# A grouped expert matmul: the first expert's loads in four buffers and on two queues, LoRA factors first, base loads later

## The reference, cut to what matters

```
w = weight[adapter_ids]
c = einsum('bsi,boi->bso', x, w)
h = einsum('bsd,nrd->nbsr', c, lora_A)
lora_out = einsum('nbsr,nor->bso', h, lora_B * (2 * lora_weights)[:, None, None])
return x + einsum('bsd,od->bso', c, W) + bias + lora_out
```

## Time and profile before

| | before |
|---|---|
| median of 3 runs | 1561.61 us (1561.08 to 1564.95) |
| profiled execution, its time | 1557.48 us |
| its span | 1555.8 us |
| TensorE busy (matmuls) | 1500.1 us, 96% |
| VectorE busy | 782.0 us, 50% |
| ScalarE busy | 386.7 us, 25% |
| POOL busy | 484.3 us, 31% |
| mean granted clock | 0.987 of full |

### The profile page before, as it was taken

How to read it: one execution, slowest core, us unless ns; L and a number is a source line. 1 busy time by engine, 2 the same in 40 slices (tenths; PEclk the granted TensorE clock), 3 DMA queues, 4 the chain that set the end, 5 groups by cost and what they waited for, 6 DMA issues and landing times.

```text
span 1555.8 us, 27863 instructions
## 1 busy us (share of the span) xinstructions
PE 1500.1 (96%) x6352; PEld 1197.8 (77%) x6353; DVE 782.0 (50%) x1183; ACT 386.7 (25%) x493; POOL 484.3 (31%) x656
## 2 busy tenths in 40 slices
PE   6779999999999999999699999999999999999998
PEld 3568788888887788887588888888888888888886
DVE  5477565675677575567773333333333333333330
ACT  3233343333334333333442101010010101010100
POOL 2743543335433334433321212121212121212221
PEclk9889999999999999999899999999999999999999
DMA  8887878778799877688866555555555555555553
GB/s 195 267 207 171 199 185 191 181 166 203 176 201 197 194 158 191 181 195 185 193 157 180 138 137 145 139 141 140 140 142 139 141 139 138 145 135 148 135 135 81
DMA packets 175346, 257.86 MB, mean 166 GB/s; under 512 B 22616, under 2 KB 131288, under 8 KB 175320
## 3 DMA queue, kind: packets, MB, share of 16 engines
q1 hardware_dynamic: 104368, 140.09, 39.2%
q10 hardware_dynamic: 50728, 72.37, 18.9%
q0 software_dynamic: 20224, 45.13, 9.9%
HBM read 181.99 MB, written 75.50 MB: 166 GB/s over the span
## 4 chain that ended last, share of the span: by engine, by line
PE 59%; issue 12%; DMA 10%; DVE 9%; ACT 3%; POOL 2%; SPq 2%; DVEq 2%; POOLq 1%; ACTq 1%
PE ps L668 20%; PE ps L670 19%; PE ps L669 19%; DMA w_raw<-in_L_cond_weight_dram 7%; DVE w_turn L487 3%; DVE w_lo L541 3%; DMA x_raw<-in_x_dram 2%; DVE x_turn L561 2%; ACT w_hi L370 1%; SPq L206 1%; POOL x_raw L193 1%; DVEq L182 1%; POOLq L182 1%; POOL fold_sb L322 1%; ACT x_hi L378 1%
## 5 line engine op out<-in xcount | busy, mean ns | idle before, releaser
L668 PE MATMUL ps<-w_hi,x_hi 128*128 (+1 forms) x2096 | 832.6, 397 | 30.8 <-ACT stage L396 13.1
L669 PE MATMUL ps<-w_lo,x_hi 128*128 (+1 forms) x2096 | 831.2, 397 | 0.0
L670 PE MATMUL ps<-w_hi,x_lo 128*128 (+1 forms) x2096 | 831.1, 397 | 0.0
L668 PEld LDWEIGHTS ps<-w_hi,x_hi 128*128 128x128 f32 x2096 | 395.4, 189 | 130.4 <-issue 23.9
L670 PEld LDWEIGHTS ps<-w_hi,x_lo 128*128 128x128 f32 x2096 | 395.1, 189 | 96.0
L669 PEld LDWEIGHTS ps<-w_lo,x_hi 128*128 128x128 f32 x2096 | 395.5, 189 | 95.5
L193 POOL DMA_DIRECT2D x_raw<-in_x_dram x560 | 300.3, 536 | 430.2 <-DVE x_turn L561 269.6
L378 ACT ACTIVATE x_hi<-x_turn 128x512 fp32r<-128x512 f32 x272 | 160.5, 626 | 798.1 <-DVE x_turn L561 475.0
L351 POOL TENSOR_TENSOR stage<-stage,w_raw 128x1024 f32<-128x1024 f32 x64 | 154.1, 2408 | 595.2 <-DMA stage<-in_x_dram 595.2
L561 DVE STREAM_TRANSPOSE x_turn<-x_raw 128x256 f32<-128x256 f32 x544 | 193.8, 414 | 177.9 <-DMA x_raw<-in_x_dram 141.5
L613 DVE TENSOR_TENSOR stage<-ps,stage 128x1024 f32<-128x1024 f32 x64 | 78.3, 1224 | 349.4 <-PE ps L670 349.4
(11 more groups left out here) (63 smaller groups left out, 27.0 us busy)
## 6 DMA issues: line engine op xcount, KB each, us to landing
w_raw<-in_L_cond_weight_dram SPq DMA_DIRECT2D x256, 256.0 KB, 5.8
y_scr<-stage ACTq DMA_DIRECT2D x144, 256.0 KB, 4.2
x_raw<-in_x_dram POOLq DMA_DIRECT2D x560, 64.0 KB, 3.2
x_raw<-y_scr SPq DMA_DIRECT2D x128, 256.0 KB, 2.7
stage<-in_x_dram SPq DMA_DIRECT2D x128, 256.0 KB, 3.7
out_dram<-stage ACTq DMA_DIRECT2D x128, 256.0 KB, 2.9
base_sb<-in_L_ffn_W_dram POOLq DMA_DIRECT2D x8, 512.0 KB, 8.9
weff<-fold_sb POOLq DMA_DIRECT2D x8, 512.0 KB, 5.4
```

The costliest lines, as they stand in the source:

```text
L668: mm(ps[b][:, cols], x_hi[b][:, t, :], hi, start=t == 0, stop=False)
L669: mm(ps[b][:, cols], x_hi[b][:, t, :], lo, start=False, stop=False)
L670: last = mm(ps[b][:, cols], x_lo[b][:, t, :], hi, start=False, stop=t == KT - 1)
```

## The change

Rank 0 gets four load buffers in place of two: the two `w_raw` and two more, `w0_raw`, which lie in memory that is used later (by `base_sb` 2 and 3, and by the last quarter of rank 1's `w_hi`, where folds 6 and 7 are put). Rank 0's loads, and the x of slots 0 and 1, are issued in two parts: partitions 0 to 63 (q = 0, 1) on SP's queue, and partitions 64 to 127 (q = 2, 3) on ScalarE's queue (loads 0 and 1) or POOL's (loads 2 and 3, and x). The row of ids moves from SP to ScalarE and the LoRA weights' coefficients from ScalarE to SP; B and A stand ahead of ScalarE's share of the loads. SP now also loads the x of slots 2, 3 and 4, ahead of rank 1's loads. POOL loads W (`load_base`) after x of slot 1, the third and fourth once six chunks are turned, and makes its eight additions without x loads between. ScalarE rounds no chunk ahead of the LoRA factor `bt_sb`, and alternates chunks and folds in another order. All experts' loads are issued in the order q = 0, 2, 1, 3.

```diff
-                   for i, at in enumerate((16, 20, 8, 12))]
+                   for i, at in enumerate((8, 12, 16, 20))]
+        w0_raw = [nc.alloc_sbuf_tensor_at(f"w0_raw{i}", [P, 2 * P // BLK, SEG], f32, offset=at)
+                  for i, at in enumerate((spare + 16 * D, base + EXPERT_BYTES + (FOLDS - 2) * 4 * D))]
...
+        first_raw = w_raw + w0_raw
...
+        def load_first(eng, c, quads, loaded):
+
+            rows = w[0][2 * c * P:2 * (c + 1) * P, :].rearrange("(m j) n -> j m n", j=BLK)
+            for q in quads:
+                eng.dma_start(first_raw[c][BLK * q:BLK * (q + 1), :, :],
+                              rows[:, :, q * SEG:(q + 1) * SEG]).then_inc(loaded[c], 16)
...
-                    if not (isinstance(k, int) and k == 0 and c < 2):
-
+                    if isinstance(k, int) and k == 1 and c < 2:
+
+                        sp.wait_ge(w_turned, 2 * (c + 1))
+                    else:
                         sp.wait_ge(w_turned, k * CHUNKS + 2 * (c - 1))
...
-                    for q in range(QUADS):
+                    for q in (0, 2, 1, 3):
...
-            sp.dma_start(row_i[:, :], ids.rearrange("(a s) -> a s", a=1).to_broadcast([P, SAMPLES])).then_inc(ids_loaded, 16)
-            load_expert(0, w[0], range(0, LOADS // 2))
+            sp.dma_start(coef[:, :],
+                         lora_weights.rearrange("(n a b) -> n a b", a=1, b=1).to_broadcast([NLORA, RANK, 1])
+                         ).then_inc(coef_loaded, 16)
+            for c in range(2):
+                load_first(sp, c, (0, 1), w0_loaded)
             sp.wait_ge(tables, 1)
             for h in range(2):
-                load_sample(sp, 0, 0, h, first_loaded[0])
-            load_expert(0, w[0], range(LOADS // 2, LOADS - 1))
+                load_sample(sp, 0, 0, h, first_loaded[0], (0, 1))
+            for c in range(2, LOADS):
+                load_first(sp, c, (0, 1), w0_loaded)
             for h in range(2):
-                load_sample(sp, 1, 1, h, first_loaded[1])
-            load_expert(0, w[0], range(LOADS - 1, LOADS))
+                load_sample(sp, 1, 1, h, first_loaded[1], (0, 1))
+            for n in range(2, RING + 1):
+                for h in range(2):
+                    load_sample(sp, n, n % 2, h, first_loaded[n % 2])
             sp.wait_ge(tables, 2)
             load_rank(1)
...
+            pool.wait_ge(tables, 1)
+            for h in range(2):
+                load_sample(pool, 0, 0, h, first_rest[0], (2, 3))
+            for c in range(2, LOADS):
+                load_first(pool, c, (2, 3), w0_rest)
+            for h in range(2):
+                load_sample(pool, 1, 1, h, first_rest[1], (2, 3))
             pool.wait_ge(b_turned, 1)
-            pool.wait_ge(x_turned, 2)
             for f in range(BASES):
+                if f == 2:
+                    pool.wait_ge(w_turned, 6)
                 load_base(f)
-            load_x(2, 0)
-            for f in range(0, 3):
-                add_base(f)
-            load_x(3, 1)
-            for f in range(3, 6):
+            for f in range(FOLDS):
                 add_base(f)
-            load_x(4, 0)
-            for f in range(6, FOLDS):
-                add_base(f)
-            load_x(5, 1)
+            load_x(RING + 1, 1)
...
-            act.dma_start(coef[:, :],
-                          lora_weights.rearrange("(n a b) -> n a b", a=1, b=1).to_broadcast([NLORA, RANK, 1])
-                          ).then_inc(coef_loaded, 16)
+            act.dma_start(row_i[:, :], ids.rearrange("(a s) -> a s", a=1).to_broadcast([P, SAMPLES])).then_inc(ids_loaded, 16)
...
+            for c in range(2):
+                load_first(act, c, (2, 3), w0_loaded)
...
-            round_w(0, 0, [0])
             act.wait_ge(b_turned, 1)
...
-            round_w(0, 0, [1])
-            move_fold(0)
-            round_w(0, 0, [2])
-            move_fold(1)
-            round_w(0, 0, [3])
+            for c in range(4):
+                round_w(0, 0, [c])
+                move_fold(c)
             round_x(0, 0)
-            move_fold(2)
-            move_fold(3)
-            round_w(0, 0, [4])
             move_fold(4)
-            round_w(0, 0, [5])
+            round_w(0, 0, [4, 5])
             move_fold(5)
-            round_w(0, 0, [6])
+            round_w(0, 0, [6, 7])
             move_fold(6)
-            round_w(0, 0, [7])
             move_fold(7)
...
             prepare_w(0, 0, range(0, CHUNKS // 2))
-            prepare_x(0, 0, 0, 0, [first_loaded], 2 * QUADS)
+            prepare_first(0)
             prepare_w(0, 0, range(CHUNKS // 2, CHUNKS))
-            prepare_x(1, 1, 1, 0, [first_loaded], 2 * QUADS)
-            for n in range(2, RING + 1):
-                prepare_x(n, n % RING, n % 2, n // 2 - 1)
+            for n in range(1, RING + 1):
+                prepare_first(n)
             prepare_w(1, 1)
```

More of the change, by code:

```diff
@@ L151, in grouped_adaln_ffn_kernel @@
         weff_ready = sem("weff_ready")
+        w0_loaded = [sem(f"w0_loaded{c}") for c in range(LOADS)]
+        w0_rest = [sem(f"w0_rest{c}") for c in range(LOADS)]
         w_loaded = [sem(f"w_loaded{b}") for b in range(2)]
@@ L157, in grouped_adaln_ffn_kernel @@
         first_loaded = [sem(f"first{b}_loaded") for b in range(2)]
+        first_rest = [sem(f"first{b}_rest") for b in range(2)]
         y_loaded = [sem(f"y_loaded{b}") for b in range(2)]
@@ L182, in entry, with load_sample @@
             return eng.value_load(table[:, bass.ds(i, 1)], min_val=0, max_val=top)
-        def load_sample(eng, n, b, h, loaded):
+        def load_sample(eng, n, b, h, loaded, quads=range(QUADS)):
             sample = entry(eng, slot_sample, 2 * n + h, SAMPLES - 1)
@@ L480, in turn_w @@
                 load, part = c // 2, c % 2
-                if part == 0:
-                    dve.wait_ge(w_loaded[load % 2], 16 * QUADS * (load // 2 + 1) + k * (16 * QUADS * LOADS // 2))
+                raw = w_raw[load % 2]
+                if isinstance(k, int) and k == 0:
+                    raw = first_raw[load]
+                    if part == 0 and load < 2:
+                        dve.wait_ge(w0_loaded[load], 16 * QUADS)
+                    elif part == 0:
+                        dve.wait_ge(w0_loaded[load], 16 * 2)
+                        dve.wait_ge(w0_rest[load], 16 * 2)
+                elif part == 0:
+                    dve.wait_ge(w_loaded[load % 2], 16 * QUADS * (load // 2 + 1) + (k - 1) * (16 * QUADS * LOADS // 2))
                 if not (isinstance(k, int) and k == 0 and c < TURN):
@@ L487, in turn_w @@
                 nc.vector.transpose(w_turn[c % TURN][:, :, :].rearrange("p t (m j) -> p m t j", j=BLK),
-                                    w_raw[load % 2][:, part * P // BLK:(part + 1) * P // BLK, :].rearrange("p m (t i) -> p m t i", i=BLK)
+                                    raw[:, part * P // BLK:(part + 1) * P // BLK, :].rearrange("p m (t i) -> p m t i", i=BLK)
                                     ).then_inc(w_turned, 1)
@@ L554, in prepare_x, with prepare_first, turn_x @@
                     dve.wait_ge(sems[raw], load * (16 * loads) + 16 * loads)
+                turn_x(n, b, raw)
+            def prepare_first(n):
+                dve.wait_ge(first_loaded[n % 2], (2 + 4 * (n // 2)) * 2 * 16)
+                if n < 2:
+                    dve.wait_ge(first_rest[n], 2 * 2 * 16)
+                turn_x(n, n % RING, n % 2)
+            def turn_x(n, b, raw):
                 for h in range(2):
@@ L576, in prepare_next_expert, with x_index @@
                     dve.nop()
+            def x_index(n):
+                return n // 2 - (2 if n % 2 else 3)
             prepare_w(0, 0, range(0, CHUNKS // 2))
[L579 removed]
+            prepare_first(0)
             prepare_w(0, 0, range(CHUNKS // 2, CHUNKS))
[L581 to L583 removed]
+            for n in range(1, RING + 1):
+                prepare_first(n)
             prepare_w(1, 1)
@@ L587, in _ @@
                 if slot > 1:
-                    prepare_x(n, n % RING, n % 2, n // 2 - 1)
+                    prepare_x(n, n % RING, n % 2, x_index(n))
                 prepare_next_expert(slot)
@@ L593, in _ @@
                     v = u + AHEAD
-                    prepare_x(slot + AHEAD, v % RING, v % 2, g * (RING // 2) + (v // 2 - 1))
+                    prepare_x(slot + AHEAD, v % RING, v % 2, g * (RING // 2) + x_index(v))
                     prepare_next_expert(slot)
```

## The result

The changed kernel took 1546.05 us (median of 4 runs, 1544.98 to 1547.09), the kernel before 1563.12 us beside it (4 runs, 1561.08 to 1564.95): ratio 0.9896, 95% interval 0.9882 to 0.991. The profiled executions stand closer together, 1557.48 and 1546.04 us (spans 1555.8 and 1543.9): before's was 5.6 us under its median, after's is on it. So 11.9 us can be followed in the traces.

What follows compares the result with a forecast made beforehand. TensorE bounds the kernel, so only its 55.7 us of standing still can be won. 21.7 us up to slot 55 (the preparation's 22.4 is larger) plus 2 before slot 67 make 23.7: 1561.6 - 23.7 = 1537.9 us, range 1529 to 1547.

Steps and rivals of the forecast that it cites:

- the later of two shifts: Whole run: TensorE and the preparation must both move early; the end shifts only by the later one's shift.
- the start up to half 0, and POOL: Slot 0 and Weff: half 0 starts at 30.2 instead of 30.52; POOL's additions end at 61.0 instead of 80.47.
- the order's size: Expert loads in order 0, 2, 1, 3: each W phase gets 0.65 us shorter.
- rival 1: Expert loads: the order gives nothing, leaving a gain of 17.2 us, 1544.4; chance 0.17.
- Rival 2: W phases: both load waits vanish, 3.5 us in each late phase; 32.2 us gained, 1529.4; chance 0.13.
- chunks 6 and 7 rounded at 39.8 and 40.9, the last `w_lo` at 42.2: Slot 0, rank 0's last chunks: ready for half 1 to start at 42.3, 8.0 us early.
- just in time: Rank 1's loads on SP: issued from 57.2 behind three x loads, landed at 66, with Weff ready at 66.5.
- my 87.2: End of rank 1's W phase: 20.7 us after Weff is ready at 66.5, shifting the preparation by 17.2 us.
- rival 3: Rank 1's loads become the wait: first lands 8 us late, phase ends at 95.2; 16.4 us gained, 1545.2; chance 0.13.
- the head: Stretch up to the end of rank 1's W phase: the preparation gets 17.2 us early there.
- fewer bytes are in flight: Argument against rank 1's loads becoming the wait: less traffic than at 50 to 58 us, when 386 GB/s moved.
- The offset: Whole run: the median of the runs is 4.1 us above the profiled execution, giving 1537.9 from 1533.8.

Runs made afterwards that it cites:

- f: Changed kernel with the eight additions done on VectorE, two behind each x of slots 1 to 4, not on POOL: 1545.07 us.
- k: Kernel before with only each expert load's order changed to 0, 3, 1, 2, which changes partition half each time: 1554.10 us.
- a: Kernel before with only each expert load's order changed to 0, 2, 1, 3: 1552.18 us.
- l: Kernel before with only each expert load's order changed to 1, 0, 3, 2, which keeps neighbours of one partition half: 1561.66 us.
- b: Changed kernel with the old order 0, 1, 2, 3 of each expert load, all else kept: 1554.47 us.
- e: Changed kernel with POOL's eight additions replaced by fills with zero, which write and don't read: 1542.02 us (1 run).
- c: Changed kernel with rank 1's first two loads issued on SP ahead of x of slots 3 and 4: 1538.62 us.
- d: Changed kernel with x of slots 3 and 4 issued on ScalarE's queue, behind the roundings of x 1 and 2: 1539.14 us.
- i: Changed kernel with rank 1's first two loads on SP right behind x of slot 1, ahead of x of slots 2 to 4: 1538.28 us.

## Why the prediction was right or wrong

**Right: that only idle time could move, and that the later of two shifts counts.** "The shift is that of the later one": half 1 moved by 2.5 us in after, 6.6 in f beyond that, and the run followed rank 1 instead. In all 14 kernels slot 6 starts 7.9 to 9.3 us after rank 1's phase ends.

**Right: the start up to half 0, and POOL.** `bt_sb` ran at 14.95 (predicted 14.4), folds from 16.12 (15.6), half 0 at 29.30 (30.2). The last addition ended at 60.41 (61.0), and Weff was no longer waited for.

**Right: the order's size.** Predicted 0.65 us a phase, measured 0.70; in all 6.5 us (21.7 - 17.2, and 2), measured 7.5 as the last column's difference between before and after (4.4 against 4.5 up to slot 55). The medians say 8.2 (k) to 9.8 (a). The part that isn't in the last column I can't place: the medians of before and l lie 4.4 to 6.4 us above their profiled executions, those of a, b, k and after between 2.8 below and 3.4 above, and there is one profile of each. The rates of two neighbouring DMAs, 217 and 191 GB/s, which gave the 0.65, seem to have been no accident; rival 1 (the order gives nothing) is refuted by a, b, k and l, and with it what the rule of the Trainium skill made of the sum. Rival 2 is refuted too: the waits became 2.67 us a phase from 3.35, they did not vanish.

**Wrong: "chunks 6 and 7 rounded at 39.8 and 40.9, the last `w_lo` at 42.2".** The roundings were done at 41.37; the last `w_lo` came at 47.78, since VectorE's subtractions waited for POOL's additions. I had moved those additions from 38–80 to 33–60 us, into the stretch where VectorE is on the path, and priced VectorE's work by its undisturbed rows. e and f take this away and half 1 starts at 42.43 and 41.22. After standing still for 5.98 us instead of 1, TensorE was granted its lower clock of 1.2 GHz at first (0.50 of full from 48 to 53), as it had been after the old stall, so slot 0 ended at 56.0 and not 47.9.

**Wrong: rank 1's loads "just in time".** They were to be issued from 57.2 and to land at 66; they were issued at 66.79, and the first chunk was turned at 75.51. The phase was counted from ScalarE's first rounding, in after:
```profile
76.86 2.13 ACT L392 ACTIVATE w_hi<-w_turn 128x1024 fp32r<-128x1024 f32 x2 [7.25 <-DVE w_turn L510]
```
Against the predicted 66.5 it is 10.4 late, and from there the phase took 23.0 us (20.7: 2.3 more), which makes the 12.6 us by which it ended after my 87.2. The 10.4 come mainly of the issue, which was 9.6 late. SP's issue of x of slots 3 and 4 waits for x of slots 1 and 2 to be turned, and behind it stand the loads. It began at 49.29 and not 43.6, since the last `w_lo` was stretched and slot 1's x was turned behind it: 5.7 us; in e, without the stretch, it began at 43.88. (The stretched `x_lo` cost the issue nothing: x of slot 2 was turned at 55.68, and SP issued slot 3's x until 56.8.) The other 3.9 us are SP's own: I took 6.4 us for 8 DMAs and 13.6 from the first of the 16 to rank 1's loads, but the 16 took from 49.29 to 65.36, and 16.8 us in e; some single ones took 0.8 to 1.2 us and not 0.57. The 2.3 us are waits inside the phase for the loads behind the first (3.96 and 1.13 us, against 2.78 in all before), which come at 209 GB/s. c and d show it: freed from x, the phase ends at 94.2 and 94.5.

**Left out: the bytes.** Even c, e and f, with one of the waits gone, ended no sooner than 94.2. I had checked each load against a landing time and never added up what must pass between 30 and 90 us. Base loads and Weff's stores are 8 MB, rank 1's matrix 4, and the x come on top: after moved 247 GB/s for those 60 us, 14.8 MB, with the DMA engines at a share of 0.90, and c 257 GB/s at 0.87. That this puts 87.2 out of reach isn't shown. Before moved 251 GB/s in the same 60 us at a share of 0.84, so the stretch was about as full then, and c moved 365 GB/s in its best 22 us. What is known is that the engines were full in c and i just where rank 1's loads and x met, and that no kernel here came near 87.2; c's order on VectorE, in which rank 1's first chunk stands behind x of slots 3 and 4, was not varied.

So **rival 3** names what happened: rank 1's loads behind x of slots 3 and 4, its phase ending at 95.2 and 1545.2 us (measured 99.84 and 1546.05). That its time agrees within 1 us is luck: its sum is 9.2 us for the head and 7.2 for the order, the traces have 4.4 and 7.5. It had a chance of 0.13. I gave it "fewer bytes are in flight" as the reason against, and had not asked what else could make their issue late.

**The offset.** I had carried the 4.1 us between profiled execution and median over to the changed kernel. Its profiled execution lies on its median, so this was no constant; forecast and result stand closer in the medians (23.7 and 17.1) than in the spans (23.7 and 11.9) for that reason alone. That the time fell inside the range is partly luck, then: the head, which was to give 17.2 us of the 23.7, gave 4.4.

## What to carry to other kernels

Before work is moved to another time, list what each engine does there, and look in the trace for instructions of the same form that take longer than their median: a mean of 1.24 us for `w_lo` in after hides the pair of 7.32 us. For a load that is moved on a queue, name what is ahead of it and what that waits for, and take the time of its issues from rows of the same busy stretch. Then sum the bytes of the whole stretch, against a rate seen for loads of the same kind: here full engines moved 209 GB/s of rank 1's loads alone and 365 GB/s of a mixture. Try the smallest part of a change alone: here one line, the order of four DMAs, was worth as much as all the rest.

## What the runs showed of the hardware

**POOL's addition blocks VectorE's subtraction.** In after seven stretched subtractions (three of `w_lo`, four of `x_lo`) end 1.08 to 1.10 us (`w_lo`) or 0.56 to 0.57 us (`x_lo`) after an addition of POOL ends, about their own length (1.18 and 0.65). So they waited, and weren't merely slowed. It can go the other way: in c, where `w_lo` ran until 42.50, the addition that began at 41.70 took 3.07 us and not 2.4. VectorE's transposes, with one input, are untouched: 1.25 us at 36.45, beside an addition at 36.75. The fills on POOL in e, which read nothing, stretched none: `w_lo` took 2.36 us for the pair beside one. This is what the Trainium skill says in "SBUF — State Buffer", section "Who interferes with whom": a VectorE instruction with two inputs in SBUF contends with a POOL instruction that reads SBUF, and whoever comes second waits for the whole of the other. I had not looked there. The rows agree with it, but they can't show who came second: three subtractions of after and the one of c are all recorded 0.40 to 0.41 us before the addition (in after one at 43.92, the addition at 44.33), and the three waited while that of c went first.

**Alternating partition halves within one queue.** DMAs of 32 partitions, 256 KB each, in one queue: a change of half at each step is worth 8 to 10 us of 1562 here; two orders that have it and two that don't show it. The Trainium skill, in "SBUF — State Buffer", section "Can I just issue two DMAs to hit both halves?", answers no, with 6% for two such DMAs side by side. The gain here is of this small kind (217 against 191 GB/s is 14% for two of four DMAs, 6% of a load); it counts because the loads of 15 experts are each waited for. The runs don't show by what mechanism it comes.
